# One ordered list for the work behind the last recurrence, and an earlier load for the first unit, in an adaLN block with a gated delta rule

## What is computed

```
sa, ca, ga, sb, cb, gb = modulation rows of silu(c) @ wmod      # ga, gb bounded away from 0
h = layernorm(x) * (1 + ca) + sa
x = x + ga * attn(h)
h = layernorm(x) * (1 + cb) + sb
x = x + gb * ffn(h)

attn: q, k, v = silu(causal conv, 4 taps, of h @ Wq, h @ Wk, h @ Wv)   # 6 heads, k 64, v 128
      q, k l2-normalised; beta = sigmoid(h @ Wb); g = -exp(A_log) * softplus(h @ Wa + dt_bias)
      per token:  S = S * exp(g);  delta = (v - k S) * beta;  S = S + k^T delta;  o = q S
      o = rmsnorm(o) * norm_weight * silu(h @ Wg);  attn = o @ Wo
ffn:  (silu(h @ w_gate^T) * (h @ w_up^T)) @ w_down^T                    # hidden width 2048
```

## Time and profile before

| | us |
|---|---|
| median of three runs | 1126.31 (1126.29 to 1127.57) |
| the profiled execution | 1130.92 |
| its span, first to last instruction | 1129.1 |
| TensorE busy | 1060.3 (94%) |
| VectorE busy | 623.2 (55%) |
| ScalarE busy | 378.3 (34%) |
| GpSimd busy | 212.0 (19%) |
| mean granted TensorE clock | 0.971 of full |

### The profile page before, as it was taken

One profiled execution on the slowest core, in us unless ns is written; L12 is line 12 of the kernel. 1 busy time (PEld: TensorE's weight loads), 2 busy tenths in 40 slices (PEclk: granted clock), 3 DMA queues, 4 the chain that ended last, 5 costly groups with the idle time before them and its releaser, 6 DMA issues.

```text
span 1129.1 us, 18642 instructions
## 1 busy us (share of the span) xinstructions
PE 1060.3 (94%) x7356; PEld 853.6 (76%) x7356; DVE 623.2 (55%) x978; ACT 378.3 (34%) x691; POOL 212.0 (19%) x166
## 2 busy tenths in 40 slices
PE   4898999999888999999887999999999999999998
PEld 2685667777676888888666788788888888888886
DVE  3775454999784677788644334233343333425356
ACT  3575555354445333334344112112121211212110
POOL 1332110011014545445321000000000000004091
PEclk8898999999899999999978999899999999999999
DMA  6502326736629465766611101001010100101223
GB/s 193 195 10 72 100 59 171 216 90 183 102 63 218 93 136 127 167 166 142 205 39 46 56 1 56 1 1 57 1 56 1 44 13 3 54 1 66 74 76 113
DMA packets 153687, 97.88 MB, mean 87 GB/s; under 512 B 93568, under 2 KB 130688, under 8 KB 153472
## 3 DMA queue, kind: packets, MB, share of 16 engines
q1 hardware_dynamic: 153600, 96.68, 31.6%
HBM read 65.19 MB, written 31.46 MB: 86 GB/s over the span
## 4 chain that ended last, share of the span: by engine, by line
PE 74%; DVE 11%; ACT 5%; issue 4%; DMA 3%; SPq 2%; POOL 1%; DVEq 0%; ACTq 0%; POOLq 0%
PE ps L1087 70%; DVE t L1682 5%; ACT t L1399 5%; DVE t L1774 3%; PE ps L1095 3%; DVE t L1687 1%; PE ps L1287 1%; SPq L967 1%; DMA t<-in_x 1%; POOL t L2136 1%; DMA t<-scrA 1%; SPq L1024 1%; ACT L1421 1%; DMA t<-scrU 0%; DVE t L1874 0%
## 5 line engine op out<-in xcount | busy, mean ns | idle before, releaser
L1087 PE MATMUL ps<-t,t 128*128 128x512 f32 (+6 forms) x6488 | 1004.1, 339 | 48.1 <-DMA t<-in_wmod 8.5
L1087 PEld LDWEIGHTS ps<-t,t 128*128 128x128 f32 (+4 forms) x6488 | 794.6, 167 | 234.5 <-issue 50.2
L1682 DVE TENSOR_TENSOR t<-ps,t 128x512 f32<-128x512 f32 (+4 forms) x306 | 208.1, 700 | 253.8 <-PE ps L1087 241.5
L1399 ACT ACTIVATE t<-t 128x512 fp32r<-128x512 f32 (+7 forms) x342 | 191.3, 579 | 338.5 <-DVE t L1682 202.9
L1682 DVE TENSOR_TENSOR t<-t,t 128x512 fp32r<-128x512 f32 (+16 forms) x209 | 162.1, 780 | 115.2 <-ACT t L1399 106.8
L1399 ACT ACTIVATE t<-ps 128x512 f32<-128x512 f32 (+5 forms) x202 | 109.8, 550 | 321.1 <-PE ps L1087 312.2
L2144 POOL TENSOR_TENSOR t<-t,t 128x512 f32<-128x512 f32 x16 | 22.5, 1407 | 406.6 <-DVE t L1682 404.5
L1774 DVE SCALAR_TENSOR_TENSOR t<-ps,t,t 128x511 f32<-128x511 f32 (+2 forms) x108 | 80.4, 747 | 20.6 <-ACT t L1399 17.8
L1095 PE MATMUL ps<-t,t 128*128 128x128 f32 (+1 forms) x388 | 59.2, 286 | 14.7 <-DVE t L1687 9.9
L1399 ACT ACTIVATE t<-ps,t 128x512 f32<-128x512 f32 (+2 forms) x96 | 56.8, 620 | 33.9 <-DVE t L1682 11.7
L1095 PEld LDWEIGHTS ps<-t,t 128*128 128x128 f32 (+1 forms) x388 | 44.3, 145 | 30.3 <-DVE t L1687 14.3
(11 more groups left out here) (49 smaller groups left out, 230.8 us busy)
## 6 DMA issues: line engine op xcount, KB each, us to landing
scrU<-t SPq DMA_DIRECT2D x60, 256.0 KB, 2.7
t<-in_wf SPq DMA_DIRECT2D x16, 768.0 KB, 4.2
t<-scrU SPq DMA_DIRECT2D x32, 288.0 KB, 4.9
t<-in_wmod SPq DMA_DIRECT2D x6, 1024.0 KB, 5.7
t<-scrU SPq DMA_DIRECT2D x32, 192.0 KB, 3.4
t<-in_W SPq DMA_DIRECT2D x19, 256.0 KB, 2.8
t<-in_x SPq DMA_DIRECT2D x16, 256.0 KB, 3.8
t<-in_x SPq DMA_DIRECT2D x32, 128.0 KB, 2.7
```

Source lines behind the costliest of these rows:

```text
L1087: return e.matmul(o, l, r_, start=start, stop=stop, skip_group_check=True)
L1399: return e.activation(o, i, f, **kw)
L1682: return e.tensor_tensor(o, a, b, op)
```

## The change

**First unit.** U of unit 0 is loaded, its `pr_gm` done and its `pr_tr` put on the list at b = 1, one projection earlier; U of unit 1 is loaded at b = 2. KgT and Kd no longer wait for U, QgT does. `rec_x` waits for `v_kd`, the step before QgT. `rec_v` of unit 0 stands ahead of `pr_kq` and waits for its U and two gate banks; `rec_q` waits for the other two. The memory of U, GMl and Sg is laid out anew.

```
@@ start_b
         elif b == 1:
             step("pr_exb", u=0, used=proj_of[1])
+            step("load_u", u=0, used=proj_of[1])
+            step("pr_gm", u=0, used=proj_of[1])
+            ringed("pr_tr", 0, ("v_kd", 1))
         elif b == 2:
-            step("load_u", u=0, used=proj_of[2])
-            step("pr_gm", u=0, used=proj_of[1])
+            step("load_u", u=1, used=proj_of[2])
...
-    step("load_u", u=1, used=proj_of[3])
     step("load_wo")
...
@@ tensor: rec_v, rec_x, rec_q
-                    for tok in gate_free:
+                    for tok in gate_free[0:2]:
                         e.wait_ge(*at_least(tok))
-                    e.wait_ge(sem("v_mg"), final["v_mg"])
+                    e.wait_ge(sem("d_u0"), 32)
...
-                e.wait_ge(sem("v_prep"), u + 1)
+                e.wait_ge(sem("v_kd"), u + 1)
```

```
+    def last_units():
+        first = products(0, 0)
+        step("po_sq", u=15)
+        mod(*ahead_of[0], "a")
+        mod_unit(*ahead_of[13])
+        step("po_ln", u=15)
+        step("po_os", u=15)
+        mod(*ahead_of[1], "a")
+        mod(*ahead_of[2], "v")
+        split(0, "p")
+        split(5, "v")
+        split(1, "p")
+        split(2, "v")
+        step("po_yg", u=14)
+        ringed("po_tr", 15, ("v_oz", 16))
+        step("po_stat", u=14)
+        tile3, tile4 = turn(3), turn(4)
+        done = [next(first)]
+        mod(*tile3, "a")
+        mod(*tile4, "v")
+        step("po_xn", u=14)
+        done.append(next(first))
+        split(3, "p")
+        split(4, "v")
+        ringed("po_wo", 15, ("v_yg", 16))
+        tile6 = turn(6)
+        done.append(next(first))
+        mod(*tile6, "a")
+        split(6, "p")
+        split(7, "v")
+        step("po_yg", u=15)
+        step("po_stat", u=15)
+        step("po_xn", u=15)
+        done.append(next(first))
+        step("table", set="silu_and_others")
+        for d in done:
+            evict_gu(*d, first_fs)
+        step("split_ff", j=2)
+        step("load_ff", j=3, wait=("v_glo", 3))
...
+        todo = (8, 9, 10, 11, 12, 13, 14, 15)
+        for i, n in enumerate(todo):
+            mod(*turn(n), "av"[i % 2])
+            if i:
+                split(todo[i - 1], "pv"[i % 2])
+            yield
...
+    order_qb = [(0, 1), (1, 0), (1, 1), (0, 2), (0, 3), (1, 2), (1, 3)]
+    order_qb += [(q, b) for q in range(2, NG) for b in range(4)]
+    for q, b in order_qb:
+        fs = []
+        for done in products(q, b):
+            evict_gu(*done, fs)
+            next(nrm, None)
```

More of the change, by code:

```diff
@@ L191, in build @@
     hf_off = c0.p
-    HF2 = [c0.new([128, 4, 128]) for _ in range(2)]
+    c0.p += 4096
     f_off = [c0.p + i * 2048 for i in range(7)]
@@ L694, in slot_of @@
             prep_1(u + 1)
+        if has_tail and u >= 15:
+            step("po_stat", u=u - 2)
         if has_rec:
@@ L702, in slot_of @@
         if has_tail:
-            step("po_stat", u=u - 2)
+            if u < 15:
+                step("po_stat", u=u - 2)
+            else:
+                step("po_xn", u=u - 2)
         if has_rec:
```

354 lines of the change are left out of this document (202 added, 152 removed).

## The result

The changed kernel takes 1120.15 us in the median of four runs (1118.28 to 1121.35), beside 1126.67 us of four runs of the kernel before: ratio 0.9939, 95% interval 0.9922 to 0.9957. So it is faster by 6 to 9 us. The forecast was 1115.0, with a range of 1110.5 to 1121.5. The profiled execution took 1119.61 us, its span is 1117.8.

What follows compares the result with a forecast made beforehand. TensorE's even product stream was taken as the bound, so time won before the 181st feed-forward product counts at the end: 13.1 − 3.0 + 1.2 = 11.3 us, profiled 1130.92 to 1119.6, median 1115.0, range 1110.5 to 1121.5.

Steps and rivals of the forecast that it cites:

- the sum behind the last recurrence: From rec_o 15 to the 181st product, full clock: work 55.1, waits 13.3, end 622.8 against 635.90, 13.1 us won.
- the five turns of the slot fall into waits of the recurrence: In slot 15, five turns made earlier cost nothing, taking 2.4 us off the work behind rec_o.
- the wait of 4.0 us: TensorE waits for the first silu before the fifth group of twelve: 4.0 us, bounds 1.5 and 8.
- The clock: Before the 181st product, one fall of TensorE's clock to its lower level, costing 3 us.
- A third fall: Listed sign of a wrong prediction: a third stretch of TensorE at the lower clock.
- Rival A: TensorE's clock stays at 2.4 GHz, no fall: 1112.0 us, chance 0.22.
- The first unit: U's load one projection earlier starts unit 0's chain up to 2.7 us earlier; Wo late next, 1.2 us won.
- From the profile to the median: Profiled execution becomes 1119.6 us; the median of three times is 4.6 lower, so it becomes 1115.0.
- B: VectorE's two splits wait fully for POOL (1.8, 1.3 us), 64-wide steps cost like 128-wide: 1117.3 us, chance 0.12.
- C: Silu wait 8 us instead of 4, or a second clock fall (2.7) behind it: 1118.5 to 1121.5 us, chance 0.15.
- D: TensorE at 1.2 GHz from the sparse stretch through 198 products to the 181st, 45 us: 1157 us, chance 0.04.
- moved weight loads or splits: Weights' loads and splits moved in the list cost nothing; without cover 2.3 us or more.

Runs made afterwards that it cites:

- silu_early: Changed kernel with po_yg of unit 15 ahead of the splits of tiles 6 and 7, unit 15's variance between them; 1110.75 us, ratio 0.9845.
- tr_filled: Kernel three with 14 added products that nobody reads ahead of po_tr of unit 15; 1107.90 us, ratio 0.9789.
- wait_filled: Changed kernel with 17 added products that nobody reads in TensorE's wait for the first silu; 1116.23 us, ratio 0.9862.
- rep_after: Changed kernel run again without an edit; 1119.68 us, ratio 0.9917 to the kernel before.
- tail_only: Changed kernel with the first unit's part undone, only the list behind the last recurrence kept; 1119.65 us, ratio 0.9926.
- first_only: Kernel before with only the first unit's part of the change; 1127.03 us, ratio 0.9980.
- best: Kernel tr_filled with pr_tr of unit 0 back behind the last projection; 1108.33 us, ratio 0.9815.
- three: Changed kernel with silu_early's reorder, unit 12's 128x64 steps later, and down (0, 0) copies ahead of the fourth late tile with other banks; 1107.67 us, ratio 0.9821.

## Why the forecast held where it did, and where it failed

**What bounds, and the sum behind the last recurrence: right, in part because two terms cancelled.** VectorE's eight 128x64 steps took 2.11 us (forecast 2.1) and `rec_o` came 2.2 us later (2.2). The first gate product comes 11.7 us behind `rec_o` (11.0). The waits are 4.07 us for silu (4.0) and 1.65 and 1.75 at `down` (1.85 each). Here is VectorE's timeline with these steps, in slot 15 and behind it:

```profile
546.86 2.11 DVE L1799 TENSOR_SCALAR t<-ps,t 128x64 f32<-128x64 f32 x8 [0.46 <-PE ps L1213]
...
554.39 2.11 DVE L1799 TENSOR_SCALAR t<-ps,t 128x64 f32<-128x64 f32 x8
...
558.56 2.35 DVE L1794 TENSOR_TENSOR t<-t,t 128x512 fp32r<-128x512 f32 x2
```

The path to silu came out step by step: from the end of `po_wo` 15, `po_yg` ended after 5.2 us (forecast 5.2) and silu began after 9.3 (9.35). One step failed without harm: "the five turns of the slot fall into waits of the recurrence". Four of them stand behind `rec_o`, 1.7 us of work (552.15 to 553.81) that was counted as gone; in return the wait of 0.9 us ahead of `po_wo` 14 is not there, and the next is 3.29 us instead of 3.9. VectorE's steps set when `po_tr` 15 may start, so `po_wo` 14 being 0.6 us later held nothing.

A layout of the list by hand with durations from the rows of before was enough for this. What it didn't ask was whether the order is a good one. It named the wait of 4.0 us with its price and left it as a fact; silu_early shows that two moved lines remove it. The 0.18 us of that kernel lie below its bound of 1.5, which was worked out for the order as it stood.

**The clock: the term was too small.** I took one fall, 3 us. In the profile of the changed kernel there were two up to the 181st product, one at `po_tr` 15 and one behind the silu wait. By tr_filled and wait_filled the first costs 1.1 us in the turns and 0.7 in the 42 products, the second 2.2: 4.0 us. I had reasoned that the wait of 4.0 us was shorter than the 6.22 ahead of before's fall and so less likely to bring one. It brought one in five profiles of five. A third fall, which the prediction names as a sign of being wrong, came in two of the six profiles that have the waits of about 1.65 and 1.75 us at `down` (rep_after and tail_only, 1.6 us each). Rival A, no fall, didn't come.

**The first unit: right, in size and in cause.** Forecast 1.2 us with Wo as what is late next; 1.1 in the first pair of profiles. In the changed kernel's two profiles Wo was issued 0.4 us later behind the silu (forecast 0.6) and landed after 6.6 and 6.8 us instead of 7.5. In the first of them `split_wo` follows without idle time, which looked like a chain on ScalarE as the limit (silu later by the six turns, table load, exponentials). But rep_after waits 1.41 us for Wo there, first_only 1.17, best 2.27, and in all of them `split_wo` comes 19.7 to 20.1 us behind the silu.

```profile
356.01 0.60 ACT L1522 ACTIVATE t<-ps 128x512 f32<-128x512 f32 x1 [0.30 <-PE ps L1205]
358.01 1.15 ACT L1522 ACTIVATE t<-t,t 128x1024 f32<-128x1024 f32 x1 [1.41 <-DMA t<-in_Wo]
```

(ScalarE's timeline of rep_after.) In the first profile the clock had fallen at `rec_d` of unit 0 (granted 0.83 from 347 to 357 us) and made the chain just as late as Wo. That fall wasn't in this run alone: it came in seven of the eleven profiles with the new first unit and in none of the three with the old one. It made the chain 1.4 to 1.6 us later, and as Wo holds `split_wo` anyway, at most 0.4 us of it arrived. The prediction had no such term, and what it fell on isn't known.

**From the profile to the median: wrong, and the largest error.** The sum gave 1119.6 us for a profiled execution, and 1119.61 was measured. That is partly luck: 0.9 us of it came from ahead of the change, and took the place of the 1.0 by which the clock's term was too small. The step that failed is "the median of the three times is 4.6 lower, and becomes 1115.0". It took three times that lay within 1.3 us as the kernel's level. Before's level is 1128.35 to 1131.91 in the four later series, 2 us and more above 1126.31, and its single runs reach from 1124.3 to 1135.9. With 1128.7 the same step would have given 1117.4, still 2.3 us under the 1119.68 measured beside it. The distance of a profiled execution from its median is no constant either: 2.2 us above in before (1128.75), 0.5 below and 1.6 above in the two profiles of the changed kernel. The measured pieces of the change, 10.4 us, agree with the ratio's interval in the larger series (6.5 to 12.2 us) but lie outside that of the first (4.8 to 8.8); why before was faster in the first series stays open.

**The rivals.** Of B, ports and sizes, the sizes were wrong (the 64-wide steps took 0.26 us each, not 0.34), the ports right in part. VectorE's two splits beside POOL's took 2.35 us together; the sum had 0.68 + 1.13 = 1.8, the rival 3.1. From the end of tile 2's modulation to the end of the splits the list had 2.3 us all the same (560.7 to 563.0), high parts of ScalarE's included, and the trace has 2.3, with no wait for them. The split of tile 7 took 1.36 us (577.83 to 579.19) where POOL's ran from 577.35 to 578.64: it ended 0.55 behind POOL's end, exactly as the one in the earlier trace rows. By the Trainium skill, "SBUF — State Buffer", Who interferes with whom, a VectorE step with two SBUF inputs contends with a GpSimd step that reads SBUF; this trace agrees, here and in the split at 567.62 us, which also ended 0.55 us behind GpSimd's. It cost 0.7 us on the chain to silu until silu_early took it off. On the table load the trace of the changed kernel again shows no further cost: 1.28 us from 582.67, silu at 583.96. C had two forms at 1118.5 to 1121.5 us, and both medians, 1120.15 and 1119.68, lie in its range and not at the likeliest 1115.0. Of its first form, a silu wait of 8 us instead of 4, nothing came. Its second, a second fall of the clock behind that wait, did come, but with 2.2 us where C had 2.7, and the first fall cost 1.8 where the sum had 3, so that both together are 1.0 us over the sum. The rest of the distance to 1115.0 is the median's step and not C. D, the clock stays low, didn't come: it was back at 2.4 GHz behind each fall. None of the moved weight loads or splits made TensorE wait, as costed.

## What to carry to other kernels

When a list is laid out anew and the layout itself shows a wait, look at what stands ahead of the step that ends it on each engine it passes: a short step on the critical chain should not stand behind work that is needed only later. A wait of some 4 us on TensorE cost another 1.6 to 2.3 us in the clock behind it, so a wait is worth more than its length. A change far up front is worth only what the next late transfer leaves of it. And three times that agree are no measure of how a kernel scatters: work from one profile to another, and give the median's offset a range of its own.

## What the runs showed of the hardware

- Idle time of TensorE between groups of products brought the granted clock to 1.2 GHz, and filler products held it up. Waits of 3.3 to 4.1 us had a fall beside or behind them in 14 cases of 14, waits of about 1.75 us in two of six. With 17 products in a wait of 4.07 us the twelve behind took 3.04 us instead of 4.6 to 5.4, with 14 in a wait of 3.8 us the small groups and 42 products took 1.8 us less. Where the idle time was filled or removed, no fall came at that place (8 cases, in six profiles).
- Four matmuls with four rows each, in a stream with no idle time, had a fall in their row or just behind it in twelve profiles of thirteen (1.6 or 3.2 us); spread out they had none in the one profile taken, but cost 1.4 us more themselves.
- The kernel before scatters over 11.5 us (67 runs), the changed one over 3.1 (10 runs), tail_only over 9.4 (9 runs), first_only over 5.8 (12 runs), `three` over 5.8 (5 runs). What makes the difference isn't settled: the two profiles of before are alike to 0.1 us in every piece, and none was taken of a run at 1124 or 1135. In the tail the one profile of first_only had shorter falls than before's two (82.8 against 83.8 us), and the start of the kernel, up to the silu of sequence 0, moves by up to 4.7 us from profile to profile, whether the kernel has the change or not.
